# Two-map landmark attention: maxima as one more contraction row, sums and averages in four column tiles

## The reference, cut to what matters

```python
xn = _rms(x, w_norm_in)
q1, q2 = (xn @ slr_wq1, xn @ slr_wq2)
k1, k2 = (xn @ slr_wk1, xn @ slr_wk2)
v = xn @ slr_wv
a1 = softmax(einsum('bqd,bkd->bqk', q1, k1) / sqrt(DH), axis=-1)
a2 = softmax(einsum('bqd,bkd->bqk', q2, k2) / sqrt(DH), axis=-1)
ctx = einsum('bqk,bkd->bqd', a1 - slr_lam * a2, v)
slr_out = ctx @ slr_wo
mixed = ssm_out + (p_medium + p_full) * slr_out        # ssm_out: a running mean over tokens
out = concatenate([mixed, xn]) @ mix_w                 # the last token also gets a landmark term
out = residual + _rms(out, w_norm_out)
out = out + 0.1 * (bus of the mean of out over tokens)
```

## Time and profile before

| what | value |
|---|---|
| median of 3 runs | 2611.19 us (2607.45 to 2611.36) |
| the profiled execution's own time | 2619.05 us |
| its span | 2616.8 us |
| busy in the span: TensorE, VectorE, ScalarE, GpSimd | 85%, 65%, 47%, 27% |
| the landmark layer | from about 1278 to 1422.65 us of the span |
| granted TensorE clock, whole span | 0.926 of 2.4 GHz |

### The profile page before, as it was taken

One profiled execution on the slowest core, in us unless ns is written; L12 is line 12 of the kernel. 1 busy time (PEld: TensorE's weight loads), 2 busy tenths in 40 slices (PEclk: granted clock), 3 DMA queues, 4 the chain that ended last, 5 costly groups with the idle time before them and its releaser, 6 DMA issues. The chain is left out here.

```text
span 2616.8 us, 30143 instructions
## 1 busy us (share of the span) xinstructions
PE 2229.1 (85%) x9848; PEld 920.3 (35%) x9888; DVE 1704.6 (65%) x2464; ACT 1217.0 (47%) x2420; POOL 698.2 (27%) x658
## 2 busy tenths in 40 slices
PE   8999999857569979877998879988878988878877
PEld 2333224312112324354454324433324436533323
DVE  5666665557877745544464664569995446569995
ACT  4655663157647753221342325346655422246653
POOL 1111110042211110121101010048981013138982
PEclk9999999968979989987957889999999999999999
DMA  4000000032000001000000000023220000022220
GB/s 162 1 1 1 1 1 1 4 46 40 11 2 1 1 23 74 1 1 1 0 1 1 1 0 1 0 74 98 87 69 1 0 1 2 1 61 92 92 81 17
DMA packets 24281, 68.64 MB, mean 26 GB/s; under 512 B 2816, under 2 KB 9024, under 8 KB 23360
## 3 DMA queue, kind: packets, MB, share of 16 engines
q1 hardware_dynamic: 23264, 65.94, 8.3%
q10 hardware_dynamic: 864, 0.79, 0.3%
HBM read 58.78 MB, written 1.57 MB: 23 GB/s over the span
## 5 line engine op out<-in xcount | busy, mean ns | idle before, releaser
L3811 POOL TENSOR_TENSOR l_drive<-l_du,l_bsb 128x1024 f32<-128x1024 f32 x126 | 296.2, 2372 | 41.2 <-DVE l_du L3712 26.3
L3563 DVE TENSOR_TENSOR_SCAN l_state<-l_decay,l_drive 128x1024 f32<-128x1024 f32 x128 | 290.2, 2280 | 10.0 <-ACT l_decay L3504 9.3
L3393 PE MATMUL l_py<-l_state,w_const 128*128 128x512 f32 x512 | 255.3, 624 | 41.4 <-DVE l_state L3571 29.8
L241 POOL TENSOR_TENSOR l_nx_small<-l_nx_small,w_norm 128x4 f32<-128x4 f32 x50 | 53.4, 1067 | 862.3 <-DVE l_nx_small L234 862.3
L403 ACT ACTIVATE l_probs<-l_psp,l_stats 128x512 f32<-128x512 f32 x256 | 173.1, 683 | 147.2 <-DVE l_stats L413 147.2
L3504 ACT ACTIVATE l_decay<-l_delta,l_a 128x511 f32<-128x511 f32 x256 | 164.9, 680 | 120.1 <-DVE l_state L3563 119.9
L1319 DVE TENSOR_REDUCE l_tops<-l_ring 128x2 f32<-128x1024 f32 x128 | 151.5, 1221 | 45.5 <-PE l_ring L1310 45.1
L411 DVE TENSOR_REDUCE l_stats<-l_psp 128x2 f32<-128x1024 f32 x128 | 156.2, 1220 | 29.2 <-PE l_psp L363 28.8
L760 DVE SCALAR_TENSOR_TENSOR l_product<-l_psu,w_gated,l_first 128x512 f32<-128x512 f32 x104 | 78.1, 751 | 132.0 <-ACT l_first L734 131.7
L1391 ACT ACTIVATE l_shared<-l_ring 128x512 f32<-128x512 f32 x256 | 139.0, 598 | 46.0 <-PE l_ring L1381 45.8
L3393 PEld LDWEIGHTS l_py<-l_state,w_const 128*128 128x128 f32 x512 | 99.9, 199 | 153.5 <-issue 86.7
(11 more groups left out here) (623 smaller groups left out, 4245.8 us busy)
## 6 DMA issues: line engine op xcount, KB each, us to landing
l_bsb<-l_rows SPq DMA_DIRECT2D x64, 512.0 KB, 3.7
l_csb<-l_rows SPq DMA_DIRECT2D x32, 256.0 KB, 3.1
l_stack<-l_parts SPq DMA_DIRECT2D x84, 64.0 KB
w_gated<-in_gated SPq DMA_DIRECT2D x1, 3297.5 KB, 10.6
w_mha<-in_mha SPq DMA_DIRECT2D x1, 2568.5 KB, 11.3
w_ssm<-in_ssm SPq DMA_DIRECT2D x2, 1171.0 KB, 14.6
w_moe<-in_moe SPq DMA_DIRECT2D x1, 2248.0 KB, 18.2
w_const<-in_const SPq DMA_DIRECT2D x1, 1131.0 KB, 13.5
```

Of the source, the lines that this page charges most:

```text
L3393: mm = pe.matmul(py[:, t, :], eye, state[:, k % STATES, t, :], start=False, stop=k % NS == NS - 1, skip_group_check=True)
L3563: dve.tensor_tensor_scan(state[:, k % STATES, :, :].rearrange("p t s -> p (t s)"), decay[:, k % 2, :, :].rearrange("p t s -> p (t s)"), dr ...
L3811: pool.tensor_tensor(drive[:, k % RING, :, :], du[:, :, :], bsb[:, k // 2 % RING, k % 2, :].unsqueeze(1).to_broadcast([P, CT, S]), ALU.mult)\
```

## The change

The exponentials are computed with the keys on the partitions, so that no map has to be turned:

- `score` and `find_top` stay, but only to get the maxima, which go to a zeroed tile `highest`. After the first batch `score` uses only pair 0 of `sc`, and waits until the maximum of the unit before it has been taken.
- `turn_top` and `take_top`: once a batch, four 128x128 matmuls against the identity put the maxima of 512 queries into rows (partitions 0, 32, 64, 96 of `top_row`).
- `score_across`: the scores a second time, keys on the output partitions, and one more contraction (`less`, -1 in one row) that subtracts the maxima: four matmuls of 32 rows a unit, in pair 1 of `sc` (both pairs for the last four units).
- `exp_scores` has neither bias nor sums. `differ`, `turn`, `take_turn`, `turn_ctx` and `take_ctx` are gone.
- `average` runs for every unit: four matmuls with 32 output partitions each (sums of both maps, v averages of both maps), side by side in four column tiles.
- `divide_ctx` now divides 64 partitions x 512 elements: a reciprocal of 512 elements a partition and a product. `project_ctx` has 64 rows; the sign and `slr_lam` are folded into `wo`.
- Means of squares (`var_in`, `var_out`) are four column tiles of 32x128 instead of one column; `eps_in` and `eps_out` are two instructions instead of one. `make_diag_out` and the next norm's copy and diagonal move from VectorE to ScalarE, a diagonal in four instructions.
- q and k are projected twice, to partitions 64 to 127 as well. GpSimd gets seven memsets.
- The steps: across at distance 5, average 6, divide 9, project 10, join and var_out 11, spread_out 12, bus and finish 13. The loop still has 26 steps.

```diff
         def score(pe, u):
-            pe.wait_ge(L["probs"].sem, L["probs"].at(0, 2 * max(u - 1, 0)))
+            pe.wait_ge(L["highest"].sem, L["highest"].at(0, u if u > TT else max(u - 1, 0)))
...
+        def score_pair(u):
+            return u % 2 if u < TT else 0
+
+        def across_pair(u):
+            return u % 2 if u >= NU - TT else 1
...
+        def turn_top(pe, b):
+            pe.wait_ge(L["top"].sem, L["top"].at(0, b + 1))
...
+                mm = pe.matmul(cx[:, b % 2, tok(t)], highest[:, b % 2, t, :, :], eye, start=True, stop=True,
+                               skip_group_check=True)
...
+        def score_across(pe, u):
+            b, t = divmod(u, TT)
+            pe.wait_ge(L["top_sb"].sem, L["top_sb"].at(0, b + 1))
+            pe.wait_ge(L["probs"].sem, L["probs"].at(0, 2 * (u - 1 if u >= NU - TT else u)))
+            for i in range(2):
+                rows = rows_of_map(t, i)
+                pe.matmul(sc[:, across_pair(u), i, :], qk[rows, 1, b, tok(t)], qk[rows, 0, b, :], start=True, stop=False,
+                          tile_position=(rows.start, 0))
+            for i in range(2):
+                rows = rows_of_map(t, i)
+                mm = pe.matmul(sc[:, across_pair(u), i, :], less[rows, :], top_row[rows, b % 2, :], start=False, stop=True,
+                               tile_position=(rows.start, 0))
+            mm.then_inc(L["across"].sem, 1)
+
+        def average(pe, u):
+            b, t = divmod(u, TT)
+            pe.wait_ge(L["probs"].sem, L["probs"].at(0, 2 * u + 2))
+            for j, a in enumerate((ones[:, 0:SH], ones[:, 0:SH], v[:, b, t, :], v[:, b, t, :])):
+                mm = pe.matmul(cx[j * SH:(j + 1) * SH, b % 2, :], a, probs[:, u % 3, j % 2, :], start=t == 0,
+                               stop=t == TT - 1, skip_group_check=True, tile_position=(0, j * SH))
             mm.then_inc(L["averaged"].sem, 1)
...
         def divide_ctx(dve, b):
-            dve.wait_ge(L["averaged"].sem, L["averaged"].at(0, b + 1))
-            dve.wait_ge(L["ctx_turn"].sem, L["ctx_turn"].at(0, b))
-            dve.reciprocal(inv[:, :], sums[:, b % 2, 0, :]).then_inc(L["inv"].sem, 1)
+            dve.wait_ge(L["averaged"].sem, L["averaged"].at(0, TT * (b + 1)))
+            dve.reciprocal(inv[2 * SH:, :], cx[0:2 * SH, b % 2, :]).then_inc(L["inv"].sem, 1)
             dve.wait_ge(L["inv"].sem, L["inv"].at(0, b + 1))
...
+            dve.tensor_tensor(ctx[2 * SH:, :], cx[2 * SH:, b % 2, :], inv[2 * SH:, :], ALU.mult).then_inc(L["ctx"].sem, 1)
```

More of the change, by code:

```diff
@@ L2196, in landmark_layer @@
     NU = B * TT
-    L = Layer(nc, name, core, ["slr"], **NextNorm.SIGNALS, **NextNorm.LAST, lam=2, chain=3, chain_sb=3,
-              sq=B, var=B, eps=B, rstd=B, diag=B, spread=B, xl=B, drive=B, ema=B, wide_q=B,
+    L = Layer(nc, name, core, ["slr"], **NextNorm.SIGNALS, **NextNorm.LAST, lam=3, blank=7, chain=3, chain_sb=3,
+              sq=B, var=B, own=B, eps=B, rstd=B, diag=B, spread=B, xl=B, drive=B, ema=B, wide_q=B,
               q=B, q_sb=B, k=B, k_sb=B, v_ps=B, v_sb=B,
               hid=1, hid_sb=2, lscore=1, arc=8, lexp=1, wide=3, logit=1, router=7, rexp=1,
-              scores=NU, highest=NU, top=NU, probs=2 * NU, ratio=2 * NU, mixp=NU, turn=NU, turn_sb=NU,
-              averaged=B, inv=B, ctx=B, ctx_turn=B, ctx_sb=B, slr=B, joined=2 * B, mix=B, sq_out=B, mix_sb=B,
-              var_out=B, eps_out=B, rstd_out=B, diag_out=B, spread_out=B, scaled=B, result=B, bus=B, bus_sb=B,
+              scores=NU, highest=NU, top=B, top_row=B, top_sb=B, across=NU, probs=2 * NU,
+              averaged=NU, inv=B, ctx=B, slr=B, joined=2 * B, mix=B, sq_out=B, mix_sb=B,
+              var_out=B, own_out=B, eps_out=B, rstd_out=B, diag_out=TT * B, spread_out=B, scaled=B, result=B, bus=B,
+              bus_sb=B,
               done=B)
@@ L2355, in turn_ctx @@
             pe.wait_ge(L["ctx"].sem, L["ctx"].at(0, b + 1))
[L2356 to L2362 removed]
+            pe.matmul(cx[:, b % 2, :], w("wo")[2 * SH:, :], ctx[2 * SH:, :], start=True, stop=True, skip_group_check=True)\
@@ L2653, in _ @@
                 for u in range(STEPS):
+                    b = batch_at(u, 4)
+                    if b is not None:
+                        turn_top(pe, b)
+                    b = batch_at(u, 11)
+                    if b is not None:
+                        join(pe, b)
+                    if 0 <= u - 5 < NU:
+                        score_across(pe, u - 5)
                     if u + 1 < NU:
                         score(pe, u + 1)
[L2656 removed]
+                    b = batch_at(u, 13)
                     if b is not None:
[L2658 to L2670 removed]
+                        bus(pe, b)
                     b = batch_at(u, 14, inner)
@@ L2673, in _ @@
                         nx.centre(pe, b)
-                    b = batch_at(u, 17, inner)
+                    if 0 <= u - 6 < NU:
+                        average(pe, u - 6)
+                    b = batch_at(u, 10)
+                    if b is not None:
+                        project_ctx(pe, b)
+                    b = batch_at(u, 11)
+                    if b is not None:
+                        var_out(pe, b)
+                    b = batch_at(u, 12)
+                    if b is not None:
+                        spread_out(pe, b)
+                    b = batch_at(u, 14, inner)
+                    if b is not None:
+                        nx.var(pe, b)
+                    b = batch_at(u, 15, inner)
                     if b is not None:
                         nx.spread(pe, b)
-                    if 0 <= u - 2 < NU:
-                        turn(pe, u - 2)
-                    b = batch_at(u, 11)
-                    if b is not None:
-                        spread_out(pe, b)
-                    b = batch_at(u, 12)
-                    if b is not None:
-                        bus(pe, b)
-                    b = batch_at(u, 15, inner)
-                    if b is not None:
-                        nx.var(pe, b)
             @block.scalar
@@ L2766, in _ @@
                 for u in range(STEPS):
+                    b = batch_at(u, 12)
+                    if b is not None:
+                        eps_out(dve, b)
+                    b = batch_at(u, 13)
+                    if b is not None:
+                        scale_out(dve, b)
+                    b = batch_at(u, 15, inner)
+                    if b is not None:
+                        nx.eps(dve, b)
                     if u < NU:
```

264 lines of the change are left out of this document (114 added, 150 removed).

## The result

The changed kernel takes 2652.06 us (median of 4 runs, 2648.21 to 2655.57) where the kernel before takes 2611.07 (2607.45 to 2611.36): ratio 1.0148, 95% interval 1.0127 to 1.0168, 41 us slower. The forecast was 2654.0.

What follows compares the result with a forecast made beforehand. TensorE was taken to set the pace, much of it at 1.2 GHz. Loop steps 41 + 32.3 + 33.2 + 29.8 + 22 = 158.3 us, with head -1.5, net +43 on 2611: 2654 us; 8 in 10 within 2625 to 2685.

Steps and rivals of the forecast that it cites:

- batch 1's period: Loop from batch 0's last average to batch 1's: division wait 5.55 us, lower clock until `join`, then upper; 32.3 us.
- the tail: Loop's end after batch 3's last average, a chain of single steps from division to `finish`: 22 us.
- the head: Before the loop: narrower means of squares take about half of 3.57 us, eps gets longer; -1.5 us (-3 to +1.5).
- step 1: The fill, second score to batch 0's last average: lower clock until average and second turn; 41 us.
- Steps 2 to 5: Rest of the loop, three batch periods and the tail, lower clock behind each division: 32.3, 33.2, 29.8 and 22 us.
- The waits: TensorE idles behind divisions: 3.7 and 4.5 us before scores in batches 0 and 1; `centre` waits 5.1 in 2 and 3.
- rival A: Upper clock all the way: step 1 loses 12 us, Steps 2 to 5 lose 4.5, 3.5, 3.5, 3.5; 2627 us; chance 0.17.
- rival D: The four column tiles of `average` run one after another, 3.4 us instead of 1.0, 16 times; 2692 us; chance 0.03.
- B: Rival: lower clock nearly all the way, since two thirds of steady passes have 32 rows; +82, 2693 us; chance 0.09.
- C: Rival: not slower; division 0.2 us instead of 3.36 and clock up; 2611 us, 2605 at best; chance 0.09.
- The streams alone don't pay: TensorE per batch: 22.7 us without any wait, against 20.4 and 21.8 before with all waits.
- The 22.7 us for a batch without any wait: TensorE per batch at upper clock: four steps 15 us, single products 6.6, small ones 1.1.

Runs made afterwards that it cites:

- Experiment 4: The changed kernel with the turn of the maxima issued as true transposes instead of products against the identity; 2666.95 us, ratio 1.0203.
- experiment 1: The changed kernel with the division's reciprocal of 64x512 sums replaced by a copy of the same elements; 2636.94 us, ratio 1.0088.
- experiment 2: The changed kernel with VectorE's next maximum and previous batch's `finish` ahead of the division, which moves directly before the joined sum; 2616.04 us, ratio 1.0024.
- experiment 5: The changed kernel with the output norm's diagonal made on VectorE again, in one instruction, instead of four on ScalarE; 2642.97 us, ratio 1.0093.
- experiment 3: The changed kernel with the across on the other copy of q and k, the score issued between its two contractions; 2649.99 us, ratio 1.0139.
- experiment 6: Three cumulative kernels on experiment 2: diagonal on VectorE and copies before exponentials; router steps later; experiment 3's rows; 2621.13, 2631.02 and 2619.43 us.
- experiment 7: experiment 2 with the diagonal on VectorE, copies ahead of the exponentials and the across on the other rows, router not moved; 2616.71 us, ratio 1.0013.
- experiment 8: experiment 7 with the maximum first in each VectorE step and `join`'s first product issued before the wait for the joined sum; 2609.30 us, ratio 0.9983.
- the first kernel of experiment 6: experiment 2 with the diagonal on VectorE and `take_mix`, the two copies, ahead of `exp_scores` on ScalarE; 2621.13 us, ratio 1.0023.
- experiment 9: The kernel before with turns of the weights as products against the identity: all turns 2615.07 us, ratio 1.0011; first five units' only 2624.28 us, ratio 1.0046.

## Why the prediction was right, and which terms were off

**The total.** 2654.0 and 2652.1 lie closer than the forecast earned. It took the layer to be 43 us longer, and "no other layer changes"; the layer grew by 42.4, but the stretch behind it was 6.9 us shorter, which the forecast put at nothing. That makes 35.5 of the 41 us between the medians. The other 5.5 are not located; the layers ahead of this one took between 1270.7 and 1283.0 us in the fourteen profiles.

**The sum.** From the second score (1304.94) to the end of the last `finish` (1461.64) are 156.7 us; the forecast said 158.3. It came out by terms that cancel. Step by step, forecast and measured: the fill 41.0 and 30.2; batch 1's period 32.3 and 37.1; batch 2's 33.2 and 33.9; batch 3's 29.8 and 31.3; the tail 22 and 24.2; the head -1.5 and -0.3 (30.36 us in the place of 30.67 from the first product to the second score). Net +43 and +42.4. That the fill's 10.8 us too much and the other terms' 9.2 too little nearly cancel is luck.

**The mis-sized term is step 1**, "all at the lower clock ... I let it rise there", behind the first average and second turn. The clock rose right behind the first turn, eight passes of 128 rows against the identity. The two steps for which 7.0 and 7.3 stood in the sum took 3.8 us each, and the score, across and score before them 4.4 where 7.1 stood. Experiment 4 shows that this turn had a part in it: as transposes, it left the clock at 0.50 for 71.7 us. It isn't enough by itself: the same turn brought the clock up at once in the changed kernel and in experiments 1, 2 and 5, but not in the six kernels of experiments 3, 6, 7 and 8, which have it too.

**Steps 2 to 5 were too short for the same clock.** Behind batch 0's division the sum lets the clock rise behind `join`, at 1351.5; it rose at about 1360.5, behind an across (3.6 us), a score, an average and a turn (1.7 to 1.9 each). From the end of `join` to there took 9.4 us where 5.95 stood, 3.5 of the 4.8 us that batch 1's period is too short. Batch 2's period came out within 0.7 us. The tail was wholly at 0.50.

**The waits** were right in place and cause. Batch 0: 3.7 forecast, 3.64 measured. Batch 1: 4.5 forecast, 2.60 measured, since the across in front of it ran at the lower clock and covered 1.9 us more. Batches 2 and 3: `centre` began 5.0 us behind the last average both times, forecast 5.1. Experiments 1 and 2 show that they were the change's main cost: without the division's length 12.7 us go, without the queue behind it 31.0 (by the loop). The forecast priced the clock behind the divisions too low, 15 us (rival A's reductions for steps 2 to 5) where experiment 2 gave back 21.8.

**Prices.** Average 0.62 and 0.60 us in two groups that overlap, 1.0 from its start to the next instruction's (L2376; forecast 1.0): the four column tiles run side by side, and rival D is out. `turn_top` 1.05 to 1.16 (forecast 0.95) at the upper clock, 2.08 at the lower (1.8). Across 1.9 and 3.6, score 0.85, `join` 1.9: as forecast. The reciprocal 3.35, at the row's end of its bounds. The four activations of the diagonal 1.27 (1.3). One price of the kernel before was read from one batch alone: the averages took 7.04 us only in the first batch, 3.76 to 4.80 in the others; it is no term of the sum.

**The head.** The sixteen passes of the earlier trace rows took 1.17 us in the place of 3.57, both at the lower clock, less than the 1.8 of the forecast. In this pair of profiles most of it was lost again to the clock: the spread products behind them took 5.32 us in the place of 3.71 (granted clock 0.51 and 0.73), and 0.3 us is all that came of it. In the six profiles where the changed head took 28.3 us it is 2.4 us shorter than the 30.7 of the kernel before. The forecast's -1.5 lies between.

**Rivals.** A, the upper clock all the way, was held off by VectorE's order around the divisions: with the order of experiment 2 the clock stood at 1.00 from 1321 to 1412, and the time was 2616. B didn't happen, the steps between stood at 1.00. C needed a short division and the clock up: with a short one the time was 2637, not 2605 to 2611, since the granted clock was 0.78 over the layer, the maximum was still queued behind two instructions and the chains of ScalarE stayed. "The streams alone don't pay" stands for the changed kernel's streams: in experiment 2, at the upper clock, a batch takes 24.9 and 25.3 us, more than the 20.4 and 21.8 before. The 22.7 us for a batch without any wait are no floor for the idea, though: with the score beside the across, experiment 8's batches take 20.8 and 21.6.

The rule that the prediction cites under A (the Trainium skill, "TensorE: Matmul & The Clock Gate", section "Part 4: PE-mode transpose") says that the upper clock doesn't engage for transposes, since they don't count as busy in the same way. Experiment 4 agrees with it, 71.7 us at 0.50 with transposes; experiment 9 gives it no support, since products in their place left the clock down for 36 and 47.8 us.

## What to carry to other kernels

Look at what is queued behind a long instruction before its length: a maximum and a `finish` that were ready stood behind a 3.35 us reciprocal, four times, and that order cost 31 us of the loop; once they went first, TensorE waited about 4 us for the division's results. Where a loop alternates between the clock's two levels, a microsecond of idle time on TensorE can cost more than itself: 12.7 us of the loop went with 9.1 of idle time in experiment 1, 31.0 with 9.2 in experiment 2. It is not a fixed rate; the 7 us of waits taken away in the first kernel of experiment 6 gave nothing. A forecast of such a loop needs its own line for the clock. Judge a small edit by its own stretch of the trace and by the medians together: the ten executions of experiment 2's kernel ran from 2613.9 to 2647.6 us, and one profile is one of them.

## What the runs showed of the hardware that was not expected

- Passes on different row tiles overlap across instructions: a score and an across's first contraction ran side by side in 1.1 us, where one after another they took 1.8 (experiment 3).
- A turn issued as transposes takes half as long as one issued as products (1.12 and 2.08 us at the lower clock) and left the clock where it was. With products the clock came up right behind the first turn in four kernels (the changed one, experiments 1, 2 and 5), 21 to 25 us behind the second score and ahead of the second turn in four (those with the score beside the across), and only during the second turn, 31 us behind, in two (experiment 6).
- Reciprocal: 3351 ns for 512 elements along a partition, 6.5 ns each, the same at 64 and at 128 partitions, against 684 ns for a copy of the same tile and 178 ns for a reciprocal of 4 elements a partition.
- The clock can stay at 0.50 for 27 us with TensorE 98% busy (experiment 6). About 8 us of that were full-height products, among them the two of `join`, behind which it had risen in the kernel before.
- The layers behind the changed one ran 4 to 8 us shorter in every profile with the new loop than in any with the old one, with the same instructions; the cause is not known.
